# A searched order of all engines, and the second attention layer of two half units as products of 32 rows

## The chip, the cores and the metric

The kernel runs on one core of a Trainium2 chip. The core has five engines that each take their instructions in order: TensorE (PE) multiplies matrices, VectorE (DVE), ScalarE (ACT) and GpSimd (POOL) work element by element, SyncE (SP) issues the transfers. The metric is the device time of one execution in microseconds, the median of several runs.

## The reference

x has two batches of 2048 rows of 128 features. Cut to what is computed:

```python
h = layernorm(x)                                  # without weights
q, k = bf16(h @ Wq.T), bf16(h @ Wk.T)             # one head of 128
q, k = rope(q), rope(k)
s = exp(q @ k.T / sqrt(128)), 0 above the diagonal
o = s.sum(axis=-1)                                # one number a row
a = relu(o * fc1_w + fc1_b) @ fc2_w.T + fc2_b     # 16 inner values
x = x + layernorm(a)
z = layernorm(x)
y = relu(z @ W1[1] + b1[1]) @ W2[1] + b2[1]       # 256 hidden values
x = x + layernorm(y)
```

The attention has no values: only the row sums of the exponentials are used. The feed-forward net is that of expert 1. The kernel folds the means of both inner layer norms and of the outputs into centred weights, so that of each norm only the squares are left.

## The kernel before

The 4096 rows are eight groups g of 512 (four tiles of 128 rows); groups 0 to 3 are batch 0, groups 4 to 7 batch 1. Each phase cuts the groups into units of its own, listed in FRONTS, BACKS and OUTS:

```python
FRONTS = [(0, 0, 2), (0, 2, 2), (1, 0, 4), (4, 0, 4), (5, 0, 4), (2, 0, 4), (6, 0, 4), (3, 0, 4), (7, 0, 4)]
BACKS = [(0, 0, 4), (1, 0, 4), (4, 0, 4), (5, 0, 4), (2, 0, 4), (6, 0, 4), (3, 0, 4), (7, 0, 2), (7, 2, 2)]
OUTS = [(0, 0, 4), (1, 0, 4), (4, 0, 4), (5, 0, 4), (2, 0, 4), (6, 0, 4), (3, 0, 4), (7, 0, 1), (7, 1, 1), (7, 2, 1), (7, 3, 1)]
```

An entry is (group, first tile, tiles). So front units 0 and 1 and back units 7 and 8 are half groups of two tiles, output units 7 to 10 are single tiles, and group 4 is unit 3 in front and unit 2 behind.

The program is a list of steps, the string STEPS (line 38). A word is `name.unit`, for scores and exponentials `name.unit.tile.segment`. `.A`, `.D` or `.P` name the engine (ACT, DVE, POOL) where several could do it, `#` the PSUM banks that it takes, out of eight. `+name` moves the result of PE step `name` out of its bank, and so frees it. Every engine walks the same list and issues its own steps in that order; a step waits on semaphores for its inputs, and a PE step also for the step that empties its bank (`Banks.free`, line 153). Nothing but this list sets the order and the engine of the work.

The steps of a front unit: `load_x`; `stat1` (statistics, DVE), `eps1` (mean square plus epsilon), `rstd1` (power -0.5, POOL), `norm1`; `tr1` (transposes of the rows, line 727), `+tr1`; `q`, `k` (products with the centred weights, line 735), `+q`, `+k` to bf16; the rope as `cos`, `sin` and their sum `rope`, where `sin` needs the halves swapped, by two transfers (`swap`, SP) or by a product (`rot`, lines 737 to 749).

A back unit: `scores` for a tile of queries against one or two groups of keys (line 761, bf16, up to 512 columns a product, and a 128-column product at line 765 that adds the mask), `exp` in place in PSUM with the row sum as a side result (ACT, line 569); `sum`; `hT` (transpose of the sums, line 772), `+hT` (first attention layer with relu, ACT); `fc2`, the second attention layer; `stat3`, `eps3`, `rstd3`, `x1` (scaled and added to x); `stat4`, `eps4`, `rstd4`, `norm4`; `trz`, `+trz`; `h0`, `h1` (the two halves of the hidden layer, line 735), `+h0`, `+h1`.

An output unit: `y` (line 810, two products of 128 columns a tile; for units 4 to 10 a bf16 product at line 800 puts the bias in first, for 0 to 3 DVE adds it, `bias`), `stat5`, `eps5`, `rstd5`, `out`, `store`. Where `out` is POOL's, DVE first scales the bank's contents (`ys`).

`fc2` reads 32 rows of h1T and of the weights for each tile. With one bank, all tiles of a unit are one product over 32 rows a tile (line 781). With two banks each bank gets half of the tiles as a product of its own (line 789): for a unit of four tiles two products over 64 rows with 256 columns. An fp32 product is two passes in the profile. Of `stat3` and `stat5`, ACT does one square a tile with the sum as a side result, DVE one statistics instruction for two tiles.

`blank` steps are products of zeros without a use for the result. `wqk`, `fc`, `w1`, `w2`, `b2` and their partners prepare the weights once.

Of the kernel before, what the change touches and what calls it, by code (L numbers as in the profile page):

```python
# [43 lines left out]
load_b2.0 stat1.7 eps1.8.A k.4#4 +k.3.A rstd1.8 norm1.6.D +q.0.A swap.3 q.4#0 eps1.2.A +k.4.A rstd1.2 norm1.8.D
tr1.6#3 +q.4.A load_table.3 cos.3.D rot.0#4 tr1.8#2 +tr1.6.A swap.4 norm1.2.D q.1#0 +tr1.8.A q.6#3 cos.4.D eps1.5.A
w2.0 b2mean.0 b2.0 sin.3.D tr1.2#2 +k.1.A rstd1.5 k.6#5 rope.3.D +q.6.A +tr1.2.A cos.0.D scores.2.2.0#3 eps1.7.A
sin.0.D scores.2.3.0#1 exp.2.2.0 k.8#2 rstd1.7 sin.4.D exp.2.3.0 scores.2.0.0#3 rope.0.D scores.2.1.0#4 +k.6.A q.8#6
rope.4.D exp.2.1.0 swap.6 norm1.5.D +k.8.A k.2#5 exp.2.0.0 cos.6.D +q.8.A scores.3.2.0#12 sum.2.D +q.1.A
scores.0.1.0#3 cos.8.D swap.8 scores.3.3.0#67 exp.0.1.0 cos.1.P +k.2.D rot.1#0 exp.3.2.0 tr1.5#4 sin.1.D q.2#3
exp.3.3.0 +tr1.5.D norm1.7.P hT.2#0 scores.3.1.0#12 +q.2.D scores.3.0.0#45 +hT.2 sin.6.D q.5#6 exp.3.1.0 swap.2  # L50
rope.1.D scores.0.0.0#0 exp.3.0.0 rope.6.D scores.0.3.0#1 load_w1.0 fc2.2#23 exp.0.0.0 sin.8.D exp.0.3.0
scores.5.0.0#45 cos.2.D +q.5.A scores.5.3.0#01 rope.8.D exp.5.0.0 k.5#7 stat3.2.D scores.0.2.0#6 exp.5.3.0 sin.2.D
# [798 lines left out]
```

How the kernel before makes its waits and increments, by code:

```python
    def until(self, engine, sem, count):  # L101
        if self.passed.get((engine, sem), 0) < count:
            engine.wait_ge(sem, count)
            self.passed[engine, sem] = count
# [221 lines left out]
        @block.sync  # L326
# [8 lines left out]
                    g, j0, tiles = FRONTS[n]  # L335
                    c = slice(j0 * P, (j0 + tiles) * P)
                    taken["q"].wait(eng, n)
                    taken["k"].wait(eng, n)
                    eng.dma_start(qk_swap[0:HALF, g, :, c], qk[HALF:P, g, :, c]).then_inc(l_swap[n], 16)
                    eng.dma_start(qk_swap[HALF:P, g, :, c], qk[0:HALF, g, :, c]).then_inc(l_swap[n], 16)
                elif name == "store":
                    g, j0, tiles = OUTS[n]
                    out_done.wait(eng, n)
                    eng.dma_start(out_v[g][:, j0:j0 + tiles], x_s[:, g, j0:j0 + tiles]).then_inc(l_out, 16)
            eng.wait_ge(l_out, 16 * len(OUTS))
# [48 lines left out]
        def sin_product(eng, n, by_half):  # L394
            g, j0, tiles, _, c = unit_of("sin", n)
            wait_table(eng, n)
            if (n,) in by_swap:
                eng.wait_ge(l_swap[n], 32)
                sine.done(rope_product(eng, n, qk_swap, qk_swap, 1, by_half), n)
            else:
                made["rot"].wait(eng, n)
# [155 lines left out]
        @block.scalar  # L557
# [22 lines left out]
                                                    bias=means[:, 2:3]), 0)  # L580
                elif name == "w2mean":
                    eng.wait_ge(l_w2, 16)
                    for h in range(HC):
```

## Time and profile before

| | us |
|---|---|
| median of 3 runs (lowest, highest) | 91.88 (91.78, 91.89) |
| the profiled execution | 91.72 |
| its span, first to last instruction | 90.0 |

| engine | busy us | share |
|---|---|---|
| PE, matmul | 82.5 | 92% |
| DVE | 76.6 | 85% |
| ACT | 71.0 | 79% |
| POOL | 56.8 | 63% |

The profile is of one execution. Starts of instructions are exact; a matmul's duration includes the way through the array, which the next one overlaps, so the distance between two starts tells what a product costs in a stream. The granted clock of TensorE is 1.00 in every stretch up to 85 us, its upper level of 2.4 GHz. "Idle before" is the time in which the engine had nothing to do ahead of an instruction, and the releaser is what it waited for.

### The profile page before, as it was taken

The page shows a single profiled execution, that of the slowest core. Times are in us where ns is not written, and L with a number is a line of the kernel's source. Part 1 is how long each engine was busy: PE and PEld are TensorE (multiplying, and loading weights), DVE is VectorE, ACT ScalarE, POOL GpSimd, SP SyncE. Part 2 cuts the span into 40 slices and gives each one's busy share as a digit, 9 for nine tenths or more (in the row PEclk, how much of TensorE's full clock was granted, in tenths as well). Part 3 has the DMA queues.
Part 4 walks back from the last instruction along what each step waited for, and adds up shares of the span by engine and source line. Part 5 has one row for each costly group of instructions (what it writes and reads, how often), then busy time and mean ns, then how long its engine had stood idle before and what let it go on. Part 6 is the DMA issues. An engine that isn't in the chain of part 4 may idle for free.

```text
span 90.0 us, 1535 instructions
## 1 busy us (share of the span) xinstructions
PE 82.5 (92%) x444; PEld 49.5 (55%) x444; DVE 76.6 (85%) x202; ACT 71.0 (79%) x210; POOL 56.8 (63%) x83
## 2 busy tenths in 40 slices
...
GB/s 26 244 240 277 312 294 170 205 15 87 149 63 123 0 117 0 60 60 0 0 0 7 0 0 0 0 0 0 53 64 11 0 120 0 0 25 149 179 246 101
DMA packets 11900, 7.64 MB, mean 85 GB/s; under 512 B 867, under 2 KB 10996, under 8 KB 11892
## 3 DMA queue, kind: packets, MB, share of 16 engines
...
q14 instruction: 5, 0.04, 0.2%
...
## 4 chain that ended last, share of the span: by engine, by line
PE 67%; ACT 20%; DMA 4%; POOL 2%; SPq 2%; issue 1%; POOLq 1%; DVE 0%
PE psum L735 24%; ACT psum L569 15%; PE psum L810 15%; PE psum L761 12%; PE psum L727 7%; DMA wqk_f<-wqk_t 4%; PE psum L789 3%; POOL rstd L505 2%; SPq L331 2%; PE psum L781 1%; ACT qk L521 1%; PE psum L710 1%; PE psum L765 1%; PE psum L772 1%; PE psum L800 1%
## 5 line engine op out<-in xcount | busy, mean ns | idle before, releaser
L505 POOL TENSOR_TENSOR rstd<-ve,half_neg 128x4 f32<-128x4 f32 (+2 forms) x38 | 34.8, 925 | 13.8 <-DVE ve L357 9.6
L569 ACT ACTIVATE psum<-psum 128x1024 f32<-128x1024 f32 (+7 forms) x48 | 36.7, 764 | 1.4 <-PE psum L761 0.6
L761 PE MATMUL psum<-qk_r 128*128 128x512 bf16 (+3 forms) x80 | 20.7, 349 | 1.4 <-ACT psum L569 0.6
L810 PEld LDWEIGHTS psum<-w_c,hid 128*128 128x128 f32 x128 | 15.6, 192 | 1.3 <-DVE cols_n L521 0.4
L735 PE MATMUL psum<-cols_n,wqk 128*128 128x512 f32 (+1 forms) x36 | 16.1, 556 | 0.0
L810 PE MATMUL psum<-w_c,hid 128*128 128x128 f32 x128 | 16.1, 278 | 0.0
L735 PE MATMUL psum<-cols_n,w_c 128*128 128x512 f32 (+1 forms) x36 | 15.6, 552 | 0.0
L761 PEld LDWEIGHTS psum<-qk_r 128*128 128x128 bf16 x80 | 6.6, 97 | 12.9 <-ACT psum L569 6.4
L727 PE MATMUL psum<-ident,rows_n 128*128 128x128 f32 x64 | 10.2, 277 | 0.1
L357 POOL TENSOR_SCALAR ve<-stats 128x4 f32<-128x4 f32 (+2 forms) x9 | 2.1, 233 | 11.6 <-DVE stats L642 6.6
L727 PEld LDWEIGHTS psum<-ident,rows_n 128*128 128x128 f32 x64 | 7.2, 141 | 3.8 <-issue 1.6
L614 ACT ACTIVATE ve<-stats,small 128x4 f32<-128x4 f32 (+1 forms) x12 | 3.6, 301 | 7.1 <-DVE stats L642 6.0
L569 ACT ACTIVATION_READ_ACCUMULATOR psum<-psum 128x1 f32 x48 | 9.2, 192 | 0.0
L675 DVE SCALAR_TENSOR_TENSOR x<-psum,rstd,x_s 128x128 f32<-128x128 f32 x32 | 9.0, 342 | 0.2
L642 DVE BATCH_NORM_STATS2 stats<-x_s 128x6 f32<-128x256 f32 x16 | 5.8, 418 | 3.5 <-DMA x_s<-x 3.5
L649 DVE BATCH_NORM_STATS2 stats<-psum 128x6 f32<-128x256 f32 x21 | 8.0, 420 | 0.8 <-PE psum L810 0.5
L621 ACT ACTIVATE rows_n<-psum 128x128 f32<-128x128 f32 x22 | 5.8, 278 | 3.2 <-PE psum L810 2.3
L735 PEld LDWEIGHTS psum<-cols_n,w_c 128*128 128x128 f32 x36 | 6.2, 191 | 3.6 <-issue 2.0
L383 POOL TENSOR_TENSOR qk_r<-qk,table 128x512 bf16<-128x512 bf16 (+1 forms) x6 | 6.1, 1043 | 2.5 <-issue 2.5
L735 PEld LDWEIGHTS psum<-cols_n,wqk 128*128 128x128 f32 x36 | 6.0, 190 | 2.4 <-issue 1.1
L521 ACT ACTIVATE cols_n<-psum 128x512 f32<-128x512 f32 (+1 forms) x11 | 5.8, 538 | 1.8 <-PE psum L727 1.5
L521 ACT ACTIVATE qk<-psum 128x512 bf16<-128x512 f32 (+1 forms) x13 | 6.6, 536 | 0.3 <-PE psum L735 0.3
...
## 6 DMA issues: line engine op xcount, KB each, us to landing
...
```

Source lines behind the costliest of these rows:

```text
L383: last = eng.tensor_tensor(dst[:, g, i, c], src[:, g, i, c], table[:, kind, t0:t0 + w], ALU.mult)
L505: ready[k].done(eng.tensor_tensor(rstd[:, g, STAT_SLOT[k], t], ve[:, g, STAT_SLOT[k], t], half_neg[:, 0:tiles], ALU.pow), n)
L521: return eng.activation(dst, src, ACT.Copy) if on_act else eng.tensor_copy(dst, src)
L569: exps.done(eng.activation(area, area, ACT.Exp, scale=scale_qk, accum_out=sums[:, g, s, j:j + 1]), n, j, s)
L621: ins = eng.activation(rows_n[:, g, j0 + j, :], area, ACT.Square, accum_out=squares(g, k, slice(j0 + j, j0 + j + 1)))
L642: ins = eng.bn_stats(pair_stats(g, k, j), source[:, g, j:j + 2, :].rearrange("p t c -> p c t"))
L649: ins = eng.bn_stats(pair_stats(g, k, j0 + j), net_pair(k, n, j))
L675: ins = eng.scalar_tensor_tensor(dst[:, g, j0 + j, :], area, rstd[:, g, STAT_SLOT[k], j0 + j:j0 + j + 1], prev[:, g, j0 + j, :], ALU.mult, ...
L727: mm = eng.transpose(bank[:, j * P:(j + 1) * P], rows_n[:, g, j0 + j, :], ident[:, :])
L735: made[name].done(eng.matmul(bank_of(name, n)[:, 0:tiles * P], weight, cols_n[:, g, c], start=True, stop=True), n)
L761: mm = eng.matmul(psum[:, own[0] + i, 0:width], query, qk_r[:, g0 + c, 1, 0:width], start=True, stop=c < gb)
L810: mm = eng.matmul(bank[:, j * P:(j + 1) * P], hid[:, g, h, (j0 + j) * P:(j0 + j + 1) * P], w2_c[:, h, :], start=not seeded and h == 0, sto ...
```

## The change

Only the list of steps changes. The core of it as a diff, in the two lines where the second attention layer of the half units stands, and the head:

```diff
-load_x.3 blank.9#7 blank.1.256#7 load_x.0 repeat.0 load_x.4 mask.0 load_wqk.0 load_fc.0 stat1.3 load_x.1 stat1.0
-eps1.3.P load_x.6 eps1.0.D stat1.4 rstd1.0 wqk.0#0 load_x.2 rstd1.3 eps1.4.A norm1.0.D load_x.8 tr1.0#1 fc.0#2
...
-eps5.0.D x1.6 eps4.5.A rstd5.0 fc2.8#0 stat4.6 rstd4.5 hT.7#2 ys.0 y.1#6 eps4.6.A +h0.4.A norm4.5.D +hT.7 out.0.P
...
-fc2.7#2 rstd5.3 x1.8 trz.6#5 stat3.7.A stat4.8 h0.5#3 +trz.6.A stat5.1.D eps4.8.P eps3.7.A h1.5#0 stat5.4.A rstd3.7
...
+load_x.0 blank.7#7 blank.1.384#7 load_x.3 mask.0 load_wqk.0 load_x.1 load_x.4 stat1.0 repeat.0 load_fc.0 eps1.0.A
+rstd1.0 stat1.3 load_x.6 wqk.0#0 eps1.3.D norm1.0.D load_x.8 rstd1.3 stat1.1 tr1.0#1 load_x.5 eps1.1.A stat1.4
...
++hT.7 norm4.5.D +h1.4.A stat4.6 fc2.8#56 stat5.3.D eps4.6.A fc2.7#23 stat3.8.A rstd4.6 trz.5#7 stat3.7.D y.4#0
```

- `fc2.7` and `fc2.8` get two banks each, so each is two products over 32 rows with 128 columns, and they stand one behind the other.
- The first loads are units 0, 3, the q and k weights, units 1 and 4, then the three small fc loads; before, they were units 3, 0, 4, the weights, the fc loads and unit 1. `blank.9` and a blank of 256 columns become `blank.7` and one of 384; two more blanks, of 256 and 384 columns, stand further on, ahead of `fc` and of `tr1.1`.
- Steps that change their engine, apart from `eps` steps. From ACT to DVE: +k.0, +trz.0, +h1.5, +h0.6, +h0.7, stat3.6, stat3.7, stat5.3. From DVE to ACT: +q.2, +trz.1, +trz.4, +trz.8, +h1.6, +h0.8, stat3.8, stat5.1. From POOL to DVE: cos.1, norm4.2, norm4.4, norm4.7. From DVE to POOL: norm1.2, norm4.1.
- The order and the banks of nearly all steps are new. The output units at the end come as 8, 7, 9, 10, before as 9, 10, 7, 8. Since the list is a line longer, line numbers of the code grow by one: line 781 for one bank becomes 782, line 789 for two banks becomes 790.

On PE, around the first scores of back unit 2, before the change. The rows with ident and rows_n are transposes (tr1), those with cols_n the products q and k, those with qk_r scores, each with its mask product behind it:

```order
L727 MATMUL psum<-ident,rows_n 128x128 x4
L735 MATMUL psum<-cols_n,wqk 128x512
L761 MATMUL psum<-qk_r 128x384
L765 MATMUL psum<-later,ident_b 128x128
L761 MATMUL psum<-qk_r 128x512
L765 MATMUL psum<-later,ident_b 128x128
L735 MATMUL psum<-cols_n,wqk 128x512
L761 MATMUL psum<-qk_r 128x128
L765 MATMUL psum<-later,ident_b 128x128
```

Here k.6 is followed at once by the scores of tiles 2 and 3. In the changed kernel, at the same place of PE:

```order
L762 MATMUL psum<-qk_r 128x256
L766 MATMUL psum<-later,ident_b 128x128
L728 MATMUL psum<-ident,rows_n 128x128 x4
L736 MATMUL psum<-cols_n,wqk 128x512
L728 MATMUL psum<-ident,rows_n 128x128 x4
L746 MATMUL psum<-qk,ident_b 128x512
L762 MATMUL psum<-qk_r 128x128
L766 MATMUL psum<-later,ident_b 128x128
L762 MATMUL psum<-qk_r 128x256
L766 MATMUL psum<-later,ident_b 128x128
L762 MATMUL psum<-qk_r 128x384
L766 MATMUL psum<-later,ident_b 128x128
```

Between k.6 (the first 512-column product after the first transposes) and the scores of unit 2 now stand the transposes of unit 2 and the rot product of unit 1; a score of back unit 0 with its mask stands ahead of the transposes of unit 8; the four tiles of back unit 2 follow each other.

On PE, behind the last score product, before the change. Rows with fc2 are the second attention layer, rows with osum hT, rows with w1_c h0 and h1, rows with w2_c y:

```order
L789 MATMUL psum<-fc2,h1T 128x256 x4
L772 MATMUL psum<-ident,osum 64x128
L735 MATMUL psum<-cols_n,w1_c 128x512 x3
L810 MATMUL psum<-w2_c,hid 128x128 x8
L781 MATMUL psum<-fc2,h1T 128x256
L772 MATMUL psum<-ident,osum 64x128
L810 MATMUL psum<-w2_c,hid 128x128 x8
L727 MATMUL psum<-ident,rows_n 128x128 x4
L800 MATMUL psum<-b2_s,ones_b 128x512
L810 MATMUL psum<-w2_c,hid 128x128 x8
L781 MATMUL psum<-fc2,h1T 128x256
L727 MATMUL psum<-ident,rows_n 128x128 x4
```

Units 5 and 6 are the first row, unit 8 and unit 7 the two rows of one product each. In the changed kernel, behind its own last score product:

```order
L773 MATMUL psum<-ident,osum 128x128
L811 MATMUL psum<-w2_c,hid 128x128 x8
L790 MATMUL psum<-fc2,h1T 128x256 x2
L728 MATMUL psum<-ident,rows_n 128x128 x4
L736 MATMUL psum<-cols_n,w1_c 128x512
L773 MATMUL psum<-ident,osum 64x128
L736 MATMUL psum<-cols_n,w1_c 128x512 x2
L773 MATMUL psum<-ident,osum 64x128
L811 MATMUL psum<-w2_c,hid 128x128 x8
L790 MATMUL psum<-fc2,h1T 128x128 x4
L728 MATMUL psum<-ident,rows_n 128x128 x4
```

The second attention layer of units 5 and 6 stood together behind the last scores; now unit 5's is ahead of them. Units 8 and 7 were one product each, with 256 columns, at two places; now they are four products of 128 columns at one place.

On DVE, from the bias of output unit 1 on, before the change. Rows of stats are statistics, rows with hid the output of the hidden layer:

```order
L690 TENSOR_TENSOR psum<-psum,b2_c 128x512
L675 SCALAR_TENSOR_TENSOR x1<-psum,rstd,x_s 128x128 x2
L642 BN_STATS stats<-x1 128x6
L649 BN_STATS stats<-psum 128x6 x2
L357 TENSOR_SCALAR ve<-stats 128x4
L675 SCALAR_TENSOR_TENSOR x1<-psum,rstd,x_s 128x128 x2
L642 BN_STATS stats<-x1 128x6
L351 TENSOR_TENSOR rows_n<-x1,rstd 128x256
L357 TENSOR_SCALAR ve<-stats 128x2
L546 TENSOR_SCALAR hid<-psum,b1_s 128x512
L675 SCALAR_TENSOR_TENSOR x_s<-psum,rstd,x1 128x128 x4
L661 TENSOR_TENSOR x_s<-psum,rstd 128x512
```

One row with hid stands there, ahead of the output of unit 3. From the same bias on in the changed kernel:

```order
L691 TENSOR_TENSOR psum<-psum,b2_c 128x512
L358 TENSOR_SCALAR ve<-stats 128x2
L352 TENSOR_TENSOR rows_n<-x1,rstd 128x512
L676 SCALAR_TENSOR_TENSOR x1<-psum,rstd,x_s 128x128 x2
L643 BN_STATS stats<-x1 128x6
L676 SCALAR_TENSOR_TENSOR x1<-psum,rstd,x_s 128x128 x2
L352 TENSOR_TENSOR rows_n<-x1,rstd 128x256
L547 TENSOR_SCALAR hid<-psum,b1_s 128x512
L643 BN_STATS stats<-x1 128x6
L676 SCALAR_TENSOR_TENSOR x_s<-psum,rstd,x1 128x128 x4
L547 TENSOR_SCALAR hid<-psum,b1_s 128x512
```

DVE now takes the output of two hidden halves there, the first of them ahead of the statistics of the half unit 7, where it took one ahead of the output of unit 3.

## Rows read from the trace of the kernel before

**Rows 1.** Page, part 1: busy us (share of the span) and count by engine
```profile
PE 82.5 (92%) x444; PEld 49.5 (55%) x444; DVE 76.6 (85%) x202; ACT 71.0 (79%) x210; POOL 56.8 (63%) x83
```

**Rows 2.** Stretches: their length, busy us by engine, PE clock, DMA
```profile
10.00:60.00 50.00, 48.61 (x249) 25.71 (x248) 47.48 (x115) 48.26 (x128) 28.47 (x35) 1.00 0.28 69
61.20:84.80 23.60, 23.60 (x145) 17.46 (x144) 20.39 (x61) 16.20 (x64) 18.18 (x21) 1.00 0.20 57
```

**Rows 3.** Chain that ended last: start, us, what; the last row from PE's timeline
```profile
35.80 0.63 PE psum L789 x4
...
50.38 0.11 PE psum L772
...
60.74 0.44 PE psum L727 x4
...
62.26 0.27 PE psum L761 x2
...
62.58 1.06 PE psum L789 x8
...
68.30 0.63 PE psum L781 x2
...
73.38 0.62 PE psum L781 x2
...
85.70 0.22 PE L800 MATMUL psum<-b_s,ones_b 128*128 128x128 bf16 x1
```

**Rows 4.** Timeline of PE: start, us, line, operation, [idle before <-releaser]
```profile
18.25 0.34 PE L761 MATMUL psum<-qk_r 128*128 128x384 bf16 x1 [0.35 <-ACT qk L521]
...
30.32 0.61 PE L761 MATMUL psum<-qk_r 128*128 128x512 bf16 x2 [0.35 <-ACT psum L569]
...
39.30 0.59 PE L761 MATMUL psum<-qk_r 128*128 128x512 bf16 x2 [0.41 <-DVE cols_n L521]
40.10 0.34 PE L761 MATMUL psum<-qk_r 128*128 128x384 bf16 x1 [0.20 <-ACT psum L569]
```

**Rows 5.** Timeline of ACT, its last exponentials (L569)
```profile
54.61 1.01 ACT L569 ACTIVATE psum<-psum 128x1024 f32<-128x1024 f32 x1 [0.60 <-PE psum L761]
...
57.93 0.80 ACT L569 ACTIVATE psum<-psum 128x768 f32<-128x768 f32 x1 [0.41 <-PE psum L765]
...
61.79 0.80 ACT L538 ACTIVATE h1T<-psum,fc 128x128 f32<-128x128 f32 x2
62.62 0.69 ACT L569 ACTIVATE psum<-psum 128x640 f32<-128x640 f32 x1
63.22 0.19 ACT L569 ACTIVATION_READ_ACCUMULATOR psum<-psum 128x1 f32 x1
```

**Rows 6.** Timeline of ACT, copies (L521) and eps (L614) of the front
```profile
11.51 0.60 ACT L521 ACTIVATE qk<-psum 128x512 bf16<-128x512 f32 x1
11.99 0.31 ACT L614 ACTIVATE ve<-stats,small 128x4 f32<-128x4 f32 x1
12.18 0.88 ACT L521 ACTIVATE qk<-psum 128x512 bf16<-128x512 f32 x2
12.92 0.33 ACT L614 ACTIVATE ve<-stats,small 128x4 f32<-128x4 f32 x1
```

**Rows 7.** Timelines of PE, DVE and PE's weight loads in the head
```profile
6.05 0.67 PE L710 MATMUL psum<-wqk_f,center 128*128 128x256 f32 x2 [1.20 <-DMA wqk_f<-wqk_t]
...
7.27 0.43 DVE L642 BATCH_NORM_STATS2 stats<-x_s 128x6 f32<-128x256 f32 x1 [0.61 <-DMA x_s<-x]
...
8.34 0.20 PEld L727 LDWEIGHTS psum<-ident,rows_n 128*128 128x128 f32 x2 [0.27 <-DVE rows_n L351]
```

**Rows 8.** DVE by stretch, and two of its groups by form (busy, mean ns)
```profile
60.00:85.00 25.00, 21.13 (x65) 1.00 0.19 54
...
L649 DVE BATCH_NORM_STATS2 stats<-psum 128x6 f32<-128x256 f32 x21 | 8.0, 420 | 0.8 <-PE psum L810 0.5 <-PE psum L789 0.2
...
L546 DVE TENSOR_SCALAR hid<-psum,b_s 128x512 f32<-128x512 f32 x7 | 5.2, 746 | 1.2 <-PE psum L735 1.0
```

More of the change, by code:

```diff
@@ L44 @@
[L44 to L52, printed above, removed]
-scores.7.1.0#45 eps3.2.P +k.5.D rstd3.2 exp.0.2.0 scores.8.3.1#01 sum.3.D swap.5 rope.2.D exp.7.1.0 tr1.7#7 cos.5.P
@@ L64 @@
-exp.6.2.1 h0.0#5 stat3.4.D eps4.1.P rstd4.1 exp.5.2.1 scores.5.2.0#01 eps3.4.D +h0.0.D scores.6.1.0#67 rstd3.4
-norm4.1.D y.2#2 exp.6.1.0 b2rows.0 x1.4 exp.5.2.0 scores.6.0.1#67 trz.1#5 stat4.4 exp.6.0.1 scores.6.1.1#01 +trz.1.D
-scores.7.1.1#34 eps4.4.P rstd4.4 scores.8.3.0#67 bias.2.D exp.7.1.1 y.0#5 stat5.2.D exp.6.1.1 norm4.4.P exp.8.3.0
-sum.5.D scores.8.2.0#01 sum.6.D eps5.2.D trz.4#3 rstd5.2 exp.8.2.0 hT.6#6 hT.5#7 +trz.4.D h0.1#4 ys.2 +hT.5
-scores.7.0.1#01 +hT.6 sum.8.D fc2.5#37 bias.0.D out.2.P exp.7.0.1 fc2.6#26 +h0.1.A stat3.5.D store.2 hT.8#0 h1.4#1
@@ new lines @@
+scores.5.1.0#67 sin.5.D fc2.3#01 eps4.2.D exp.1.3.0 rope.5.D q.7#2 rstd4.2 stat3.3.D exp.5.1.0 sum.0.D scores.4.2.0#45
+eps3.3.D +q.7.D rstd3.3 k.7#3 exp.4.2.0 norm4.2.D hT.0#2 scores.1.0.0#67 +k.7.D +hT.0 scores.1.1.0#45 x1.3 exp.1.0.0
+swap.7 cos.7.P fc2.0#23 exp.1.1.0 scores.5.1.1#6 scores.4.0.0#01 stat3.0.D exp.5.1.1 trz.2#7 stat4.3 exp.4.0.0
+scores.4.1.1#4 scores.7.0.0#56 eps3.0.P +trz.2.D rstd3.0 exp.7.0.0 sum.1.D scores.4.1.0#01 eps4.3.D sin.7.D h1.2#7
+rstd4.3 x1.0 exp.4.1.1 exp.4.1.0 scores.8.2.1#56 scores.5.3.1#4 +h1.2.D norm4.3.P scores.4.2.1#2 scores.4.3.1#3
@@ new lines @@
+exp.6.3.1 eps4.1.D eps3.4.P y.2#6 rstd3.4 exp.6.2.0 rstd4.1 x1.4 exp.5.0.1 scores.6.1.1#23 scores.5.2.0#45 bias.2.D
+exp.6.1.1 norm4.1.P scores.8.3.0#01 y.0#7 stat5.2.D exp.5.2.0 stat4.4 eps5.2.P exp.8.3.0 rstd5.2 sum.5.D hT.5#4
+trz.1#5 eps4.4.P +hT.5 ys.2 scores.8.2.0#23 rstd4.4 +trz.1.A scores.7.0.1#01 sum.6.D exp.8.2.0 bias.0.D fc2.5#46
+out.2.P b2rows.0 h0.1#5 exp.7.0.1 stat3.5.D scores.7.1.1#23 norm4.4.D store.2 hT.6#0 y.3#1 exp.7.1.1 eps3.5.P
+stat5.0.D rstd3.5 +hT.6 eps5.0.P x1.5 rstd5.0 fc2.6#02 sum.8.D trz.4#3 stat3.6.D h1.1#4 +trz.4.A bias.3.D eps3.6.A
```

54 lines of the change are left out of this document (30 added, 24 removed).

## The prediction

> **What bounds the kernel now.** I read the page's busy shares first, then the table by stretch, then TensorE (PE) in order of time. The page gives PE 92%, DVE 85%, ACT 79% [rows 1]. The averages hide two regimes. From 10 to 60 us ACT works 48.3 and DVE 47.5 of 50 us; from 61.2 to 84.8 us PE is never idle, while ACT works 16.2 and DVE 20.4 of 23.6 us [rows 2]. So first the exponentials on ACT pace everything. Then the feed-forward products that could not be done beside them run on PE back to back. In the chain that ended last every piece from 61 us to 84.8 is PE work, and the last output product starts at 85.70, 4.3 us before the span ends [rows 3]. That last stretch (square, eps, power, scaled sum, store) is the same chain in both orders.
>
> Two instants therefore decide: T, when PE has finished its last score product (62.58 now, where the next piece begins, 27.4 us before the end), and how much PE work stands behind it. Ahead of T, PE has four visible waits, 0.35, 0.35, 0.41 and 0.20 us, 1.3 in sum; three of them are for ACT [rows 4]. ACT itself idles 0.60 and 0.41 us for PE shortly before its last exponential, which ends at 63.41 [rows 5]. The two engines hand each other waits; neither alone is the bound.
>
> **The products of 32 rows.** Today fc2.8 and fc2.7 are one product of 64 rows and 256 columns each, two passes in fp32. They take 0.63 and 0.62 us of the chain [rows 3]: 1.25 in a dense stretch. The other units, where two products of 64 rows run side by side in two banks, show where it goes: one unit, four passes, takes 0.63 as well, and two units behind each other take 1.06, so the second adds 0.43 [rows 3]. So a pass of 256 columns takes 0.22 us, two row groups at once cost no more, and about 0.2 us is paid once for entering and leaving. With 128 columns a pass takes half, 0.11; both units now stand next to each other, so four pairs of passes give 0.44 + 0.2 = 0.64 us against 1.25. I take **-0.6 us**. The bounds of this term: if 32-row products do not pair, eight passes in series cost 0.88 + 0.2 = 1.08, saving 0.2. If each also shows its weight load, another 0.11 each by the same pace, it is 1.96 and a loss of 0.7. I stay near the full gain because the paired 64-row rows are the nearest form. The Trainium skill (TensorEngine Tiling (Array Packing), Tiling Modes) says different row tiles load and multiply in parallel, but that changing the tiling mode drains TensorE. By that rule the 0.2 us is the drain, and it is paid once where the new order has it once; the trace agrees on the parallel part, and no row here shows 32 rows.
>
> **Work behind the last score product.** In the new order hT.6 and trz.4 come behind it (0.11 + 0.44) and fc2.5 goes ahead of it (1.06 - 0.63 = 0.43) [rows 3]. Everything else behind it is the same set. Net +0.1, with the products -0.5: 26.9 us from T to the end.
>
> **T, from ACT.** ACT's queue up to its last exponential loses two of six eps steps of the first norm (0.19 each, from 11.99 to 12.18), +k.0 (0.26: half as wide as the 0.48 of 11.51 to 11.99, and 12.92 - 12.18 - 0.48), +trz.0 (0.48) and +hT.6 (0.35: a pair takes 0.80, one 0.45), and gains +q.2 and +trz.1 (0.48 each) [rows 5, 6]: -0.38 - 0.26 - 0.48 - 0.35 + 0.96 = **-0.5 us**. With as much idle time as now the last exponential ends at 62.9. The three last are 8.2.0, 7.0.1 and 7.1.1; the last two take 0.7 and 0.8, so 8.2.0 ends at 61.4 and frees banks 2 and 3 for the last score product, which needs 0.3 to 0.4 (62.26 to 62.58) [rows 3, 5]. T cannot be before 61.8 unless ACT's own idle 1.0 us goes as well; then 60.8.
>
> **T, from PE.** Ahead of T PE has 0.1 us less (above) and two more fillers, of 256 and 384 columns, 0.27 us, since the last score product's 512 and 128 columns take that [rows 3]. What counts is its waits. The one at 18.25 is for ACT's +q.6, which empties bank 3 for the first score of back unit 2. Now that bank comes from k.1, emptied long before, and tr1.2 and rot.1 stand between k.6 and the score, 0.44 us and more of work. I count 0.35 us gone. Score pairs on banks 6, 7 still alternate with exponentials of 1.0 us, so of the other 0.96 I expect half to come back elsewhere; fillers eat 0.27. That is -0.1 - 0.35 - 0.5 + 0.27, about -0.7, so PE would allow 61.9, and ACT allows 61.8. As every hand-over among three nearly full engines must hold for that, I take a little over half of it: **T = 62.2**.
>
> **The head** I cost at nothing, from -0.6 to +0.5 us. Unit 0 is now loaded first. Today the first weight product waits 1.20 us for its load, fourth in the queue [rows 7], now third. That brings unit 0 perhaps a microsecond forward. But the stream that follows runs on unit 3's normalization, which PE awaits at 8.34 (0.27 us) [rows 7]. On DVE it now stands behind the statistics of units 1 and 4, whose loads moved back behind the weights; today DVE waited 0.61 us for unit 1's load [rows 7]. So the gain stops there. On PE fc.0 stands ahead of k.0 and waits for the small fc loads, which also moved back; its cover is the microsecond by which k.0 could be early. On SP the load of w1 now stands ahead of the first swap; it is issued before q.3 is ready, and if not, sin.3 is late by one issue.
>
> **DVE's last 25 us.** DVE works 21.1 of 25 us there [rows 8]. It takes over +h0.6, +h1.5, stat3.6, stat3.7 and stat5.3 and gives up +h1.6, stat3.8 and stat5.1; the half-size pair +h0.7 and +h0.8 cancels, and so do the copies trz.4, trz.8 against norm4.4, norm4.7. Net that is one 512-wide output, 0.75, and 2 + 1 + 2 - 1 - 2 = 2 statistics of 0.42 [rows 8]: +1.6 us, 22.7 of 25. I cost it at nothing because ACT's squares, 1.0 us a unit, are gone in exchange and PE needs each result only a few steps on. Placed by hand behind T at the distances above, norm4.7 ends 0.6 us before trz.7, and bank 5 is free 0.4 us before y.5. That is the cover; past it each microsecond costs one.
>
> **The sum.** 62.2 + 26.9 = 89.1 us span, against 90.0. The profiled execution took 91.72, so 1.7 lies around the span: 90.8. The median of the runs is 0.16 above the profiled one: **91.0 us**, against 91.88.
>
> **Rivals.**
> - *ACT's idle goes too.* PE comes early enough that exponentials never wait: T = 60.8 to 61.8, time 89.7 to 90.7. For: both idles of ACT [rows 5] are waits for PE. Against: then DVE, at 95%, must also run ahead.
> - *The order gives nothing, the products do.* New waits for ACT replace the four: T = 62.6, time 91.4; if the head also slips by 0.4, 91.8, no change. For: ACT is at 97% in [rows 2] whatever the order. Against: its queue is shorter by 0.5.
> - *Slower: DVE becomes the bound of the last 25 us.* +h1.5 stands ahead of stat4.7, from which norm4.7 and trz.7 hang. If DVE's 1.6 us more show on PE from 0.4 us of lateness on, and T stays at 62.2, the end is 1.2 us later: 92.2; with the head's slip 92.6. For: DVE's idle there is only 3.9 us, in pieces. Against: the cover above, and ACT has 1.5 us less.
> - *32-row products don't pair.* 0.4 lost: 91.4; at the worst bound 92.3.
>
> **How the numbers follow.** Forecast (90.6 to 91.4) 0.45. ACT's idle goes 0.15. Products alone or no change 0.17, of it half within 0.2% of 91.88, which is about what a measurement of this kernel can tell from no change. Slower by DVE 0.17. No pairing 0.06, of it 0.04 faster. Faster: 0.45 + 0.15 + 0.09 + 0.04 = 0.73; same 0.09; slower 0.18. Range 90.2 to 92.0: it leaves out the deep end of the first rival (0.08) and most of the slower case (0.12).
>
> **What the profile would show.** Right: the line of the 32-row products with two starts together and about 0.64 us from the first of eight passes to the next transposes; the last score product done near 62.2; PE without a wait from there to the last output product near 84.8; no wait for ACT in front of the first scores of back unit 2. Wrong: PE waits for DVE between 75 and 85 us (the slower case), or waits of half a microsecond and more for ACT on banks 6 and 7 between 25 and 45 us with T at 62.6 or later. It fails altogether if the first transposes of unit 3 start later than 9 us.

## The result, and the profile after

The changed kernel takes 93.88 us in the median of five runs (93.48 to 95.15), the kernel before 91.89 beside it (91.78 to 93.08): 1.0253 times as long, 95% interval 1.0212 to 1.0294. It is slower by 2 us, where 91.0 was forecast. Runs of one kernel lie up to 4.5 us apart here (one of 290 us stands alone), so each experiment below is told by its median and lowest run and by its ratio to the kernel before on the same chip, and the ratio leaves out runs far above the kernel's fastest (for e4 it rests on three runs of twelve).

The profiled execution took 94.68 us with a span of 92.9. The page, part 1 and the chain's shares by engine:

```profile
PE 83.5 (90%) x443; PEld 51.0 (55%) x448; DVE 76.7 (82%) x201; ACT 70.7 (76%) x204; POOL 58.0 (62%) x83
...
PE 49%; ACT 17%; DVE 8%; DMA 7%; POOL 6%; SPq 5%; issue 3%; POOLq 1%
```

The busy times of PE, DVE, ACT and POOL are those of [rows 1] to within 1.2 us (the weight loads, PEld, to 1.5), so the loss is waiting, and PE's extra microsecond is of the size of the products at half pace shown below. A quarter of the chain is VectorE, transfers, GpSimd and SyncE's queue. Stretches of the changed kernel, with columns as in [rows 2]:

```profile
5.00:8.00 3.00, 1.55 (x9) 0.93 (x8) 2.36 (x7) 0.84 (x3) 2.37 (x3) 0.96 0.91 263
8.00:11.00 3.00, 3.00 (x11) 2.12 (x11) 2.72 (x9) 0.60 (x1) 2.01 (x2) 0.50 1.04 289
...
10.00:60.00 50.00, 47.79 (x234) 25.43 (x237) 44.35 (x108) 46.96 (x125) 28.08 (x31) 0.99 0.28 68
...
60.00:85.00 25.00, 24.42 (x163) 18.25 (x163) 21.53 (x61) 17.78 (x62) 18.11 (x25) 1.00 0.12 33
69.80:88.50 18.70, 18.70 (x126) 14.85 (x124) 16.28 (x49) 13.32 (x54) 14.24 (x19) 1.00 0.21 58
```

Against [rows 2] ACT and DVE have 1.3 and 3.1 us less work done by 60 us. PE is without a gap only from 69.8 us on, not from 61. And from 8 to 11 us the granted clock is 0.50, the lower level of 1.2 GHz, behind three microseconds in which PE was busy for 1.55.

The head on PE, against [rows 7]:

```profile
4.79 0.67 PE L711 MATMUL psum<-wqk_f,center 128*128 128x256 f32 x2 [0.19 <-DMA wqk_f<-wqk_t]
...
7.43 0.35 PE L718 MATMUL psum<-fc_f,repeat 17*128 17x2 f32 x2 [1.16 <-DMA fc_f<-fc_wb]
7.64 0.67 PE L719 MATMUL psum<-fc_f,repeat 17*128 17x128 f32 x2
8.24 1.22 PE L736 MATMUL psum<-cols_n,wqk 128*128 128x256 f32 x2
9.26 1.06 PE L728 MATMUL psum<-ident,rows_n 128*128 128x128 f32 x4
```

The weight product comes 1.3 us earlier than before, as intended. Then PE waits 1.16 us for the small fc loads. k.0 (8.24) and the first transposes of unit 3 (9.26) then run at half pace: 1.22 and 1.06 us for what takes 0.70 and 0.64 at the upper level, in the run with the early load below. This is the profiled execution, one of two of the five whose mean granted clock is 0.982 (94.68 and 95.15 us). The other three have 0.990 to 0.999 and still took 93.48 to 93.88 us, so this fall of the clock is not the whole loss of the median run.

The second place is SyncE's queue and ScalarE behind it, then PE behind ScalarE:

```profile
14.92 0.52 SPq L340 DMA_DIRECT2D qk_swap<-qk  x1
15.48 0.60 SPq L341 DMA_DIRECT2D qk_swap<-qk  x1
16.12 0.59 SPq L325 DMA_DIRECT2D b_f<-b  x1
```

```profile
19.90 0.31 ACT L595 ACTIVATE spare<-b_f 128x128 f32<-128x128 f32 x1 [1.40 <-DMA b_f<-b]
...
20.84 0.39 PE L746 MATMUL psum<-qk,ident_b 128*128 128x512 bf16 x1 [1.07 <-ACT cols_n L522]
```

swap.3 has to wait for the copy of q.3, which ScalarE ends at 14.89, and load_b2 stands behind it. swap.3 is issued 2.0 us later than in the kernel before (12.88). The load, issued at 16.12, lands at 19.88, and b2mean, ScalarE's first use of it, waits 1.40 us. The chain has the transfer as one of its longest pieces, "16.12 3.76 DMA b_f<-b".

The third place is around the last score product. VectorE, from b2rows on through stat3.5 (65.00) to x1.5 (67.67), then PE:

```profile
63.43 1.10 DVE L683 COPY b_s<-b_h 1x128 bf16<-1x128 bf16 x1
...
64.75 0.22 DVE L685 CAST b_s<-b_r 1x128 bf16<-1x128 f32 x1
65.00 0.76 DVE L650 BATCH_NORM_STATS2 stats<-psum 128x6 f32<-128x256 f32 x2
...
67.67 1.13 DVE L676 SCALAR_TENSOR_TENSOR x<-psum,rstd,x_s 128x128 f32<-128x128 f32 x4 [0.51 <-POOL rstd L506]
```

```profile
65.03 0.28 PE L773 MATMUL psum<-ident,osum 128*128 128x128 f32 x1
...
67.66 0.66 PE L728 MATMUL psum<-ident,rows_n 128*128 128x128 f32 x4
68.85 1.13 PE L736 MATMUL psum<-cols_n,w_c 128*128 128x512 f32 x2 [0.53 <-DVE x L676]
...
73.66 0.71 PE L790 MATMUL psum<-fc,h1T 32*128 32x128 f32 x8
74.30 0.66 PE L728 MATMUL psum<-ident,rows_n 128*128 128x128 f32 x4
...
88.50 0.22 PE L801 MATMUL psum<-b_s,ones_b 128*128 128x128 bf16 x1
```

I take T here as the start of the next product behind the last score product: 65.0, against 62.5 before. From there it is 27.9 us to the end of the span, before 27.5. The last output product starts at 88.50. h1.1 starts 1.19 us after the transposes ahead of it, a distance of 0.5 when nothing waits. h1.1 takes bank 4, which fc2.5 filled and x1.5 empties. x1.5 hangs from stat3.5 through GpSimd's power step, and ahead of stat3.5 stand the three copies of b2rows (lines 683 to 685), 1.57 us from 63.43 to 65.00, of which 1.10 is one copy. The products of 32 rows are 0.64 us from their first pass to the next transposes.

### The profile page after: what moved, and what is told of

It is laid out like the page before. It is cut to its first block, busy times and chain, and to the rows that moved or that the text cites. A ratio compares the mean times of both kernels' runs of the same rounds, so it can differ in the third digit from the quotient of the medians.

```text
span 92.9 us, 1532 instructions
## 1 busy us (share of the span) xinstructions
PE 83.5 (90%) x443; PEld 51.0 (55%) x448; DVE 76.7 (82%) x201; ACT 70.7 (76%) x204; POOL 58.0 (62%) x83
## 4 chain that ended last, share of the span: by engine, by line
PE 49%; ACT 17%; DVE 8%; DMA 7%; POOL 6%; SPq 5%; issue 3%; POOLq 1%
PE psum L736 22%; ACT psum L570 13%; PE psum L811 8%; PE psum L762 7%; POOL rstd L506 5%; PE psum L728 5%; DMA b_f<-b 4%; DMA fc_f<-fc_wb 3%; PE psum L790 3%; DVE stats L650 2%; DVE x L676 2%; SPq L332 2%; POOL ve L358 1%; PE psum L766 1%; DVE psum L691 1%
## 5 line engine op out<-in xcount | busy, mean ns | idle before, releaser
L506 POOL TENSOR_TENSOR rstd<-ve,half_neg 128x4 f32<-128x4 f32 (+2 forms) x38 | 36.3, 960 | 20.8 <-DVE ve L358 14.6
L762 PE MATMUL psum<-qk_r 128*128 128x512 bf16 (+3 forms) x75 | 19.6, 346 | 1.1 <-ACT psum L570 0.6
L736 PE MATMUL psum<-cols_n,wqk 128*128 128x512 f32 (+1 forms) x36 | 17.0, 588 | 0.0
L522 ACT ACTIVATE cols_n<-psum 128x512 f32<-128x512 f32 (+1 forms) x13 | 6.9, 527 | 7.0 <-PE psum L728 6.9
L728 PEld LDWEIGHTS psum<-ident,rows_n 128*128 128x128 f32 x64 | 8.0, 148 | 4.6 <-issue 2.5
L650 DVE BATCH_NORM_STATS2 stats<-psum 128x6 f32<-128x256 f32 x23 | 8.6, 419 | 0.4 <-PE psum L790 0.3
L615 ACT ACTIVATE ve<-stats,small 128x4 f32<-128x4 f32 (+2 forms) x13 | 3.9, 297 | 5.4 <-DVE stats L643 4.6
L547 DVE TENSOR_SCALAR hid<-psum,b_s 128x512 f32<-128x512 f32 (+1 forms) x9 | 6.4, 716 | 0.9 <-PE psum L736 0.7
L766 PE MATMUL psum<-later,ident_b 128*128 128x128 bf16 x32 | 6.8, 219 | 0.1
L358 POOL TENSOR_SCALAR ve<-stats 128x4 f32<-128x4 f32 (+2 forms) x12 | 3.5, 294 | 5.3 <-DVE stats L650 3.9
```

What stands on the lines that cost most here:

```text
L506: ready[k].done(eng.tensor_tensor(rstd[:, g, STAT_SLOT[k], t], ve[:, g, STAT_SLOT[k], t], half_neg[:, 0:tiles], ALU.pow), n)
L522: return eng.activation(dst, src, ACT.Copy) if on_act else eng.tensor_copy(dst, src)
L547: ins = eng.tensor_scalar(hid[:, g, h, c], src[:, 0:w], b1_s[:, h:h + 1], 0.0, ALU.add, ALU.max)
L650: ins = eng.bn_stats(pair_stats(g, k, j0 + j), net_pair(k, n, j))
L728: mm = eng.transpose(bank[:, j * P:(j + 1) * P], rows_n[:, g, j0 + j, :], ident[:, :])
L736: made[name].done(eng.matmul(bank_of(name, n)[:, 0:tiles * P], weight, cols_n[:, g, c], start=True, stop=True), n)
```

## The experiments

The theory after this reading is that three steps cost the time, and none of them is the one I feared: the wait for the fc loads with the slow clock behind it, load_b2 behind swap.3, and b2rows ahead of stat3.5. The rival is that they only show where full engines meet, and that taking one away brings the next. Line numbers of the experiments are one less than those of the changed kernel. Each diff shows the words of the list that move.

| run | median (lowest) us, runs | ratio to before, 95% |
|---|---|---|
| changed kernel | 93.88 (93.48), 5 | 1.025 (1.021 to 1.029) |
| e1 fc loads first | 94.37 (93.26), 6 | 1.022 (1.015 to 1.029) |
| e2 b2mean late | 92.44 (91.68), 12 | 1.003 (0.998 to 1.007) |
| e3 both | 93.41 (92.50), 6 | 1.016 (1.009 to 1.023) |
| e4 one bank | 94.05 (91.97), 12 | 1.008 (1.002 to 1.015) |
| e5 b2 load early | 92.57 (91.58), 11 | 1.004 (0.999 to 1.009) |
| e6 b2mean, b2rows late | 91.58 (90.80), 13 | 0.994 (0.990 to 0.998) |
| e7 b2mean late, filler | 92.00 (91.67), 12 | 1.000 (0.997 to 1.003) |
| e8 all three | 92.12 (91.07), 12 | 0.999 (0.995 to 1.003) |
| e9 all three, one bank | 92.03 (91.50), 12 | 1.001 (0.998 to 1.004) |
| e10 filler alone | 92.66 (92.12), 13 | 1.008 (1.005 to 1.011) |
| e11 b2 load early, filler | 92.33 (91.34), 12 | 1.000 (0.996 to 1.005) |
| e12 e11 and b2rows late | 91.05 (90.62), 12 | 0.990 (0.985 to 0.994) |
| e13 fc.0 behind k.0 | 91.41 (90.39), 12 | 0.989 (0.984 to 0.995) |
| before, load of b2 late | 93.61 (92.08), 12 | 1.006 (1.001 to 1.011) |
| before, b2rows late | 92.89 (92.58), 12 | 1.007 (1.003 to 1.011) |
| before, filler | 92.10 (91.56), 12 | 1.002 (1.000 to 1.004) |

### The head: fc loads, and the bias load

e1 moves the fc loads:

```diff
 load_wqk.0
+load_fc.0
 load_x.1 load_x.4 stat1.0 repeat.0
-load_fc.0
```

> The changed kernel with one step moved: the three small fc loads go right behind the q and k weights on SyncE, ahead of the loads of units 1 and 4; nothing else. Theory A (the head's late fc load, and the halved clock that follows the idle TensorE, carry a good part of the loss): fc.0 starts near 6.3 us and not at 7.4, the granted clock stays 1.00 from 8 to 11 us, tr1.3 starts near 8.3 and not at 9.26, and the end comes about 1.3 us earlier: 92.5. Rival B (the loss is the sum of small waits among three full engines anywhere before the last score product; what the head gives is taken back by the next wait): head earlier as in A, but 93.6 to 94.1.

The gain did not come: 94.37. fc.0 starts at 6.39, but PE waits again two steps on, for unit 3:

```profile
7.07 0.70 PE L735 MATMUL psum<-cols_n,wqk 128*128 128x256 f32 x2
8.47 1.11 PE L727 MATMUL psum<-ident,rows_n 128*128 128x128 f32 x4 [0.71 <-DVE rows_n L351]
```

The loads that were moved back again are those of units 1 and 4. Unit 4 lands at 7.04 in place of 6.53, and VectorE waits 0.93 us for it ahead of unit 3's normalization. The granted clock is 0.50 here too, from 9 to 11 us, now behind this wait. My theory named a right cost and the wrong cure; here one load became early at the expense of another.

e2 takes the wait for b2 away by moving its first use, e5 by moving its load:

```diff
 sin.3.D k.6#4
-b2mean.0
 +tr1.8.A
...
 h1.0#7 stat4.1
+b2mean.0
 b2.0 exp.6.0.0
```

```diff
 cos.0.D w2.0
+load_b2.0
 swap.3
...
 q.4#5
-load_b2.0
 eps1.5.A
```

> The changed kernel with one step moved: b2mean, ScalarE's first use of the second layer's bias, goes from its place at about 19.9 us to right ahead of b2, past 40 us; nothing else. Theory A (ScalarE's 1.40 us wait for that load at 19.90, and the 1.07 us of TensorE behind it, reach the end, since ScalarE paces this stretch): ScalarE doesn't wait there, the rot product of unit 1 starts about 1.2 us earlier than 20.84, and the end comes 1.0 to 1.4 us earlier: 92.5 to 92.9. Rival B (VectorE is already the later engine there, by its own waits of 1.5 and 1.4 us for the copies of q and k, so ScalarE's wait is covered): 93.6 to 93.9.

> The changed kernel with one step moved on SyncE: load_b2 right ahead of swap.3, as in the kernel before, and no longer behind it; b2mean stays at its place on ScalarE. Theory A (the load queued behind a swap that waits for the copy of q.3 is what makes ScalarE wait 1.4 us): b2 lands before 17 us, ScalarE has no wait for it at 19.9, and the time is that of the run with b2mean moved late, 92.2 to 92.7. Rival B (the gain of that run came from b2mean's 0.4 us of work and its place, not from the load): 93.6 to 93.9. Rival C (its gain was the spread of the head): any median between 92.5 and 94 with as wide a spread as the other runs.

92.44 and 92.57, against 93.88: two different edits of the same link give back 1.4 and 1.3 us by the medians, as theory A said, and 2.1 and 1.9 by the ratios. Rival B of e5 is out, for b2mean kept its place and its 0.4 us there. Rival C, the spread of the head, is not out by this alone, since 92.57 and runs from 91.58 to 94.04 fit it too. The pairs with the filler below (e10 against e7 and e11) settle it. e5's profile has no wait on ScalarE in front of b2mean, at 16.82:

```profile
16.82 0.30 ACT L594 ACTIVATE spare<-b_f 128x128 f32<-128x128 f32 x1
```

Its head also happened to be early, since the fc loads landed at 6.55 and not at 7.29 as in the changed kernel's profile:

```profile
6.69 0.35 PE L717 MATMUL psum<-fc_f,repeat 17*128 17x2 f32 x2 [0.61 <-DMA fc_f<-fc_wb]
...
7.29 0.70 PE L735 MATMUL psum<-cols_n,wqk 128*128 128x256 f32 x2
7.83 0.64 PE L727 MATMUL psum<-ident,rows_n 128*128 128x128 f32 x4
...
8.00:11.00 3.00, 2.98 (x13) 1.59 (x13) 2.96 (x9) 2.30 (x9) 2.61 (x3) 1.00 1.15 292
...
61.88 0.22 PE L765 MATMUL psum<-later,ident_b 128*128 128x128 bf16 x1
```

So an order that differs in the first 60 us by that load alone reaches T = 61.9, where the changed kernel has 65.0. These are the fastest run of e5 (91.58) and one above the median of the changed kernel (94.68), so the 3.1 us are more than the edit is worth. The two traces, step by step, show how the 3.1 us build up: the copy of tr1.3 starts 1.84 us later in the changed kernel (10.35 against 8.51), that of q.3 2.08 (14.30, 12.22), b2mean 3.08 (19.90, 16.82), the first exponential of unit 3 2.82 (25.26, 22.44), that of 7.0.0 3.05 (43.04, 39.99). Of the difference between these two runs about two thirds is the head, a third the bias load, and hardly anything is lost or won behind it.

> The changed kernel with both moves of the two runs before: the fc loads right behind the weights, and b2mean right ahead of b2. If the head and the late bias load are separate links of one chain, their gains add: 91.0 to 91.4. If they share what is late next (VectorE), the sum gives little more than the larger one alone: 92.3 to 92.7. Rival B of both: 93.6 or more.

e3 joins e1 and e2: 93.41. It doesn't add up, since e1's half is no gain: PE waits 0.93 us for unit 3's rows at 8.57.

e7 fills PE's wait in place of shortening it, with b2mean late as in e2; e10 has the filler alone:

```diff
-blank.1.256#7
+blank.4#7
 load_w2.0 fc.0#2
```

> The changed kernel with b2mean right ahead of b2, and the product of zeros ahead of fc.0 made longer: four of 512 columns for one of 256, some 0.75 us more of TensorE in the 1.2 us in which it waits for the small fc loads. Theory A (what the halved clock takes at 8 to 11 us is lost up to the end, and it comes from TensorE's idle time ahead of it): the granted clock is 1.00 from 8 to 12 us in the profile, tr1.3 is done 0.5 us earlier than in the changed kernel, and the runs spread less and lie at 92.0, 0.4 below the run with b2mean alone. Rival B (the fillers only displace products that were ready, or the clock is covered by the waits for loads): 92.4 or more, with the same spread.

> The changed kernel with the longer product of zeros ahead of fc.0 alone; the load of b2, b2mean and b2rows stay as in the changed kernel. Theory A (the late head with its halved clock and the late bias load are linked: an earlier q.3 means an earlier swap.3 and so an earlier b2): q.3 is copied near 13.0 and not 14.9, b2 lands near 18 and not 19.9, ScalarE waits well under 1.4 us, and the time is 92.4 to 92.8 with a small spread. Rival B (the bias load costs its 1.4 us whatever the head does): 93.3 to 93.6.

With b2mean late, 92.00 against 92.44 (by the ratios 1.000 and 1.003, whose intervals overlap), and the runs draw together: the twelve lie between 91.67 and 92.39, where e2's twelve go up to 95.99. The mean granted clock is 0.994 or more in all twelve. Alone, the filler gives 92.66, 1.2 less than the changed kernel (1.6 by the ratios). It also tells the wait from the pace, for fc.0 starts at 7.43 as in the changed kernel, and k.0 only 0.17 us earlier (8.07), but the products behind it are at the upper level:

```profile
8.61 0.60 PE L727 MATMUL psum<-ident,rows_n 128*128 128x128 f32 x4
```

0.65 us are won up to here, and 1.45 up to the copy of q.3: the price of the head in that profile is the pace, and hardly the wait itself. And it shows that the two links are one chain: q.3 is copied from 12.85 on, b2 lands at 17.91, and ScalarE's wait is smaller:

```profile
17.93 0.31 ACT L594 ACTIVATE spare<-b_f 128x128 f32<-128x128 f32 x1 [0.89 <-DMA b_f<-b]
```

Its runs still go up to 94.34, so the small spread of e7 is not the filler's alone. With the filler in, the bias load is worth 0.7 us: 1.008 (1.005 to 1.011) for e10 against 1.000 for e7 (0.997 to 1.003) and for e11 below (0.996 to 1.005). That is less than the 1.9 to 2.1 without it, so the prices of single edits overlap and must not be added.

e13 lets nothing wait for the fc loads (with the early load of b2 and b2rows late):

```diff
-blank.1.256#7
+blank.3#7
...
-fc.0#2
 k.0#1
+fc.0#2
```

> The changed kernel with load_b2 right ahead of swap.3, b2rows right ahead of x1.5, fc.0 moved on TensorE from ahead of k.0 to behind it, and three products of zeros of 512 columns for one of 256 at its old place. Theory A (fc.0 at that place makes everything wait for the small loads; behind k.0 nothing waits): k.0 starts at 6.9 to 7.2 and not at 8.24, transposes of unit 3 before 8.4, q.3 copied near 12.4, all runs close together at 91.0 to 91.2. Rival B (the head's gain stops at unit 3's normalization, which is ready near 8.0 in any case): the time of the run before it with the filler, 91.3.

91.41 (90.39 to 92.76), beside e12 with 91.05 (90.62 to 91.93). Rival B holds: k.0 comes 0.6 us earlier, at 7.16, but the transposes of unit 3 stay at 8.42, where e12 has them at 8.29.

### b2rows

e6 adds to e2:

```diff
 out.2.P
-b2rows.0
 h0.1#5 exp.7.0.1 stat3.5.D ... rstd3.5 +hT.6 eps5.0.P
+b2rows.0
 x1.5
```

> The changed kernel with b2mean right ahead of b2 (as in the earlier run), and besides b2rows, three small copies on VectorE, moved from ahead of stat3.5 to right ahead of x1.5, so that they no longer stand in front of the statistics from which the second hidden half of unit 1 hangs through VectorE's queue. Theory A (the 1.1 us by which TensorE starts h1.1 late are b2rows' 1.5 us on VectorE): h1.1 starts within 0.2 us of the transposes ahead of it, the last score product to the end takes 27.0 and not 27.9 us, and the time is 0.8 to 1.0 below the run with b2mean alone (92.44): 91.5. Rival B (norm4.4 and GpSimd's power step are next): gain under 0.3: 92.2 to 92.5.

> The changed kernel with all three edits that helped singly: b2mean right ahead of b2, b2rows right ahead of x1.5, and the longer product of zeros ahead of fc.0. Theory A (three separate causes, gains add): the time of the run with b2rows moved, 91.58, less the 0.4 to 0.5 that the filler gave: 91.1, that is 0.9 us below the kernel before, and a spread as small as with the filler. Rival B (with the head early VectorE or ScalarE is late next and takes it back): 91.5 to 91.7.

91.58 for e6, 0.86 less than e2, as theory A said. But e8, the same step on top of e7, gave 92.12, nothing less than e7's 92.00, though its lowest run is 0.6 lower (91.07, 91.67). In its profile the tail is cured, and T is 0.8 us later than e7's (63.6 against 62.8): fc.0 started 0.55 later (7.54, 6.99), and the rest arose between 41 and 47 us. So the sum was open. A pair on one chip that differs in b2rows alone tells it:

> The changed kernel with load_b2 right ahead of swap.3 on SyncE, as in the kernel before, and the longer product of zeros ahead of fc.0; b2mean and b2rows where the changed kernel has them. Theory A (what is left of the loss is only b2rows, 0.7 to 1.0 us): last score product at 61.9 to 62.8, 27.8 us from there to the end, 92.0. Rival B (ScalarE's 0.4 us for b2mean in the crowded front costs too): 92.4.

> As the run with the early load and the filler, and b2rows on VectorE moved from ahead of stat3.5 to right ahead of x1.5. Theory A (b2rows' 1.5 us ahead of stat3.5 reach the end through h1.1, since TensorE is never idle behind it): 0.7 less than that run, 91.2 to 91.4, and 27.1 us from the last score product to the end. Rival B (the two earlier results differ by chance and b2rows is covered): the same time, 92.0.

92.33 and 91.05: 1.3 us, more than the 0.7 I expected, by the ratios 1.0, in the lowest runs 0.7 (91.34, 90.62). The two profiles are further apart than the edit makes them: up to 60 us the orders are the same, yet T is 63.4 in e11 and 61.8 in e12. Most of that is one transfer of a swap, issued at 22.65, which took 3.96 us where e12's took 2.35:

```profile
26.64 0.69 DVE L386 TENSOR_TENSOR qk_swap<-qk_swap,table 128x1024 bf16<-128x1024 bf16 x1 [1.11 <-DMA qk_swap<-qk]
```

VectorE and PE in e12:

```profile
60.59 0.76 DVE L649 BATCH_NORM_STATS2 stats<-psum 128x6 f32<-128x256 f32 x2 [0.28 <-PE psum L789]
...
62.54 0.17 DVE L682 COPY b_s<-b_h 1x128 bf16<-1x128 bf16 x1
...
63.21 1.13 DVE L675 SCALAR_TENSOR_TENSOR x<-psum,rstd,x_s 128x128 f32<-128x128 f32 x4
```

```profile
61.77 0.22 PE L765 MATMUL psum<-later,ident_b 128*128 128x128 bf16 x1
...
64.45 0.65 PE L727 MATMUL psum<-ident,rows_n 128*128 128x128 f32 x4
64.94 1.02 PE L735 MATMUL psum<-cols_n,w_c 128*128 128x512 f32 x2
...
69.62 0.71 PE L789 MATMUL psum<-fc,h1T 32*128 32x128 f32 x8
```

h1.1 follows its transposes by 0.49 us without a wait, where e11 has 1.19 with 0.54 of it idle. From T = 61.8 on PE has no gap:

```profile
61.90:84.50 22.60, 22.60 (x154) 17.86 (x153) 19.92 (x62) 15.22 (x58) 16.63 (x23) 1.00 0.21 59
```

The span is 88.9 us, 27.1 of it behind T, and TensorE's share of the chain is 73%, where the changed kernel has 49. e12 is the version that beats both kernels: 0.990 times the kernel before, and no run of twelve above 91.93, 1.5 us below the fastest of the changed kernel.

### The same faults put into the kernel before

```diff
-load_b2.0
...
 swap.3
+load_b2.0
```

> The kernel before with one step moved on SyncE: load_b2 right behind swap.3 instead of ahead of it. Theory A (a load behind a swap costs what ScalarE then waits at b2mean): swap.3 is issued at 12.1 to 13.3 us here, so b2 lands about 4 us later, at 17.3 or more, b2mean can't start at 16.62, ScalarE waits 0.7 to 1.2 us, and as ScalarE paces this stretch the time grows by that: 92.6 to 93.1. Rival B (the wait is absorbed by the waits that follow): 91.9.

A ratio of 1.006, with a lowest run 0.7 us above the lowest of the unchanged kernel beside it (92.08, 91.41); the medians, 93.61 against 92.18, are further apart. So the wait costs here as well, a little less than the 0.7 to 1.2 expected if the ratio is believed. The load lands at 20.15, not near 17.3 as expected, for this profile is of a run of 95.33 us in which the whole head up to 13 us is at half pace (the last section) and swap.3 is issued at 15.60. b2mean waits:

```profile
20.18 0.31 ACT L594 ACTIVATE spare<-b_f 128x128 f32<-128x128 f32 x1 [0.66 <-DMA b_f<-b]
```

```diff
-b2rows.0
...
+b2rows.0
 stat3.5.D
```

> The kernel before with one step moved: b2rows from 55.0 us on VectorE to right ahead of stat3.5 at 63.3. Theory A (at that place it delays x1.5 and with it h1.1): its three copies take 0.6 us, or 1.5 if GpSimd's sum runs beside them as in the changed kernel; h1.1 follows x1.5 by three engines, TensorE has 0.3 us of other work at hand, so the end is 0.4 to 1.0 later: 92.3 to 92.9. Rival B (covered): 91.9.

Every run is above 92.5, where the lowest of before beside it is 91.71: +0.9 by the lowest runs, +0.6 by the ratio. In the profile stat3.5 begins at 64.20 in place of 63.26, and PE first waits at 69.37:

```profile
62.99 0.74 DVE L682 COPY b_s<-b_h 1x128 bf16<-1x128 bf16 x1
...
69.37 0.30 PE L772 MATMUL psum<-ident,osum 128*64 128x128 f32 x1 [0.60 <-DVE x L675]
```

Not at h1.1, as I had expected, but at hT.7, whose bank x1.6 empties, and x1.6 stands behind x1.5 on VectorE. The mechanism is the expected one, at another bank.

```diff
-blank.1.256#7
+blank.5#7
 load_x.0 ... load_wqk.0
```

> The kernel before with the 256 columns of zeros ahead of wqk lengthened to five products of 512, some 1.0 us of its 1.2 us wait for the weights. Theory A (its few runs near 93 are those in which TensorE's clock is halved in the head): no run with a mean clock under 0.98, fastest runs unchanged at 91.6, median 91.8. Rival B (those runs have another cause): the same share of them.

92.10 (91.56 to 92.37), and none of its twelve runs has a mean clock under 0.99, where 8 of the 36 of the kernel before beside it had 0.981 or less, all of them 92.9 us or more. Twelve such runs in a row would come by chance about once in twenty times, so that the filler takes the slow clock away here as well is likely and not shown; the median doesn't fall, as the weight load of wqk itself starts 0.4 us later (6.41 in place of 6.02).

### The products of 32 rows

e4 is the changed kernel, e9 is e8, each with one bank a unit:

```diff
-fc2.8#56
+fc2.8#5
...
-fc2.7#23
+fc2.7#2
```

> The changed kernel with the second attention layer of units 8 and 7 back in one bank each (64 rows, 256 columns, four passes in series instead of eight of 128 columns in pairs); order and everything else as in the changed kernel. If my term for the products of 32 rows is right, the four passes take about 4 x 0.22 + 0.2 = 1.1 us where the eight take 0.64, and since TensorE has no wait behind them up to the last output product, the end comes 0.4 to 0.5 us later: 94.3. Rival: TensorE has room behind, and VectorE or ScalarE set the end: within 0.1 of the changed kernel.

> The kernel with all three edits, and the second attention layer of units 8 and 7 back in one bank each: 64 rows, four passes of 256 columns, in place of eight passes of 128 columns in pairs. With a steadier head than in the earlier run, the difference to the kernel with all three edits is the price of the products alone. Theory: 0.42 us in TensorE's stream (1.06 against 0.64 from the first pass to the transposes behind), and all of it at the end: 91.5. Rival: covered, same time as the kernel with all three edits.

The same place in e4, then in e8:

```profile
74.36 1.13 PE L781 MATMUL psum<-fc,h1T 64*128 64x256 f32 x4
75.42 0.66 PE L727 MATMUL psum<-ident,rows_n 128*128 128x128 f32 x4
```

```profile
71.43 0.71 PE L789 MATMUL psum<-fc,h1T 32*128 32x128 f32 x8
72.07 0.66 PE L727 MATMUL psum<-ident,rows_n 128*128 128x128 f32 x4
```

1.06 against 0.64 (1.05 in e9): in the traces the price is 0.42 us, and it stands unchanged at the end (the last output product is 1.12 us later in e4 than in the changed kernel, of which 0.70 was there before fc2.8). The times don't tell it: medians of 94.05 against 93.88 and 92.03 against 92.12, lowest runs of 91.50 against 91.07 in the second pair. The spread of the runs is larger than the effect. One of e4's twelve runs took 91.97 us with all three faults in (the next is 93.08), so what the faults cost differs from run to run.

## Why the prediction was wrong, point by point

- **The products of 32 rows: right.** 0.64 us from the first of eight passes to the next transposes, as forecast, at 1.25 before [rows 3]. By e4, 0.42 of the 0.6 is the narrower rows and 0.2 the two units standing together.
- **Work behind T: right in the work, wrong in the wait.** 27.9 us from T to the end, where I had 26.9. The net +0.1 of moved products held to 0.1 us, as e12 shows (27.1 against 27.5 before, where I summed -0.5). That PE would find h1.1 ready was never argued. I compared the fc2, hT and h products of the two orders, not what VectorE has to do between fc2.5 and x1.5. The order itself showed b2rows moved from 55 us to just ahead of stat3.5. e12 without that has no wait there.
- **T from ACT and from PE: right in the best runs only.** I took 62.2. e5 and e12, whose first 60 us are those of the changed kernel but for the load of b2 and the filler, have 61.9 and 61.8; both profiles are of their kernel's fastest run. e7, e8, e9, e11 and e13, with b2 out of the way and no fall of the clock, have 62.8 to 63.6. The queue of ScalarE is as much shorter as I summed: 55.0 us of work up to the end of the last exponential, against 55.6 before. That the hand-overs among three full engines would hold was the weak part, as a transfer 1.6 us longer shows in e11. The wait at the first score of unit 2 [rows 4] was to go; in its place came 1.07 us a few products earlier, for ScalarE, and behind that the load.
- **The head, costed at nothing between -0.6 and +0.5: this step failed.** It was worth about 2 us up to the copy of q.3 in the profiled run, and 1.2 us of the median by e10 (1.6 by the ratios). I did name the wait of fc.0 for the moved-back loads, and set its cover at the microsecond by which k.0 could be early. That held within my range: k.0 was 0.46 us later than before (8.24 against 7.78). What I did not cost is what TensorE's clock does behind the idle time: the half clock from 8 to 11 us. e10, where fc.0 starts at the same 7.43 and the clock does not fall, shows it. The condition I gave for failing altogether, transposes of unit 3 later than 9 us, was met at 9.26.
- **load_b2 behind swap.3: missed.** For SyncE I weighed the move of w1 ahead of the first swap and not the move of b2 behind it, a load whose user is near. 1.3 to 1.4 us by the medians of e2 and e5, 0.7 with the filler in.
- **The slower rival: not what happened.** VectorE's work from 60 to 85 us is 21.5 us (22.0 from 62.5 to 87.5, as everything came 2.5 us later), not the 22.7 I summed [rows 8], and PE never waits behind 69.8 us. VectorE was late once, by a step that is preparation of weights.
- The sum, 62.2 + 26.9 = 89.1 us of span and 90.8 for the profiled run, is near what e12 shows in its fastest run, 61.8 + 27.1 = 88.9 and 90.62, and the 91.0 of time near its median of 91.05. The forecast described the order without its three faults. That it comes so near is partly luck, for the two terms err by -0.4 and +0.2, and e12 also has the longer filler.

Shown is the whole: with the three causes removed the loss is gone (e12, 0.990 against 1.025). Left open: how it divides among the three, since single edits overlap; why the gain of b2rows was missing in e8 and 1.3 us in e12 (0.7 is what PE's wait in the traces explains); what besides a late transfer moves T from 61.8 to 63.6; and whether e7's small spread needs both of its edits.
